# Expert stage of a fused two-layer kernel: first product in 512 columns, next expert's numbers read between blocks, output tiles signalled singly

## The reference

```python
cap = int(CAP_FACTOR * B * S / E)
t = x.reshape(-1, D)
probs = jax.nn.softmax(t @ Wr, axis=-1)
idx = jnp.argmax(probs, axis=-1)
...
ein = disp.reshape(E, cap, D)
h = jax.nn.relu(jnp.einsum('ecd,edf->ecf', ein, W1))
eout = jnp.einsum('ecf,efd->ecd', h, W2).reshape(E * cap, D)
...
x = x + jnp.tanh(g_ffn[1]) * _L1_ffn_ref(_layernorm(x, axis=-1), L1_ffn_Wr, L1_ffn_W1, L1_ffn_W2)
```

## Time and profile before

| | us |
|---|---|
| median of 3 runs | 2019.31 (2018.92 to 2020.88) |
| the profiled execution | 2018.42 |
| span of its profile | 2016.7 |
| TensorE busy | 1920.3 |
| VectorE busy | 953.5 |
| ScalarE busy | 742.3 |
| GpSimd busy | 759.5 |

### The profile page before, as it was taken

The page is one execution under the profiler, slowest core; times in us unless marked ns, Lnnn a source line. Parts: engine busy times, 40 slices in busy tenths (PEclk is TensorE's granted clock), DMA queues, the critical chain, the costliest instruction groups (busy, mean ns, idle before and its releaser), DMA issues.

```text
span 2016.7 us, 34799 instructions
## 1 busy us (share of the span) xinstructions
PE 1920.3 (95%) x10956; PEld 1630.0 (81%) x10957; DVE 953.5 (47%) x2245; ACT 742.3 (37%) x1711; POOL 759.5 (38%) x803
## 2 busy tenths in 40 slices
PE   5899999999999389999999999999999999999997
PEld 3677777777776279898899989998898998899986
DVE  6879999999985733324121332124133214121331
ACT  3446666666565322414111231124123114111331
POOL 5656675675652322415211241124224115211340
PEclk9999999999999699999999999999999999999999
DMA  7323443533534551505201250115124115101220
GB/s 241 110 87 126 158 148 126 174 132 126 183 122 166 169 174 55 175 29 171 76 27 35 65 169 26 36 42 173 52 72 157 31 32 183 52 31 31 92 75 11
DMA packets 152911, 208.79 MB, mean 104 GB/s; under 512 B 13472, under 2 KB 79264, under 8 KB 152839
## 3 DMA queue, kind: packets, MB, share of 16 engines
q1 hardware_dynamic: 111767, 114.15, 17.9%
q0 software_dynamic: 15728, 43.38, 7.1%
q10 hardware_dynamic: 25344, 50.33, 7.0%
HBM read 140.98 MB, written 68.37 MB: 104 GB/s over the span
## 4 chain that ended last, share of the span: by engine, by line
PE 82%; DVE 7%; issue 5%; ACT 1%; DVEq 1%; DMA 1%; POOL 1%; SPq 0%; ACTq 0%; POOLq 0%
PE bank L782 25%; PE bank L790 24%; PE bank L1527 7%; PE bank L1445 7%; PE bank L750 6%; PE bank L730 6%; PE bank L1499 2%; DVE x2T_lo L1855 1%; PE bank L708 1%; PE bank L739 1%; PE bank L1453 1%; DVE xdT_lo L1855 1%; DMA stage<-in_L_ffn_W_dram 1%; DVE a_m L1874 0%; DVE up_lo L1846 0%
## 5 line engine op out<-in xcount | busy, mean ns | idle before, releaser
L890 DVE SCALAR_TENSOR_TENSOR hT_lo<-bank,hT_hi 128x256 fp32r<-128x256 f32 x352 | 149.4, 424 | 678.6 <-ACT hT_hi L658 677.6
L658 ACT ACTIVATE hT_hi<-bank 128x256 fp32r<-128x256 f32 x352 | 134.9, 383 | 754.0 <-PE bank L782 744.5
L782 PE MATMUL bank<-inT_hi,w_hi 128*128 128x256 f32 x1408 | 399.7, 284 | 0.6 <-DVEq L938 0.6
L782 PE MATMUL bank<-inT_hi,w_lo 128*128 128x256 f32 x1408 | 400.0, 284 | 0.0
L782 PE MATMUL bank<-inT_lo,w_hi 128*128 128x256 f32 x1408 | 396.7, 282 | 0.0
L790 PE MATMUL bank<-w_hi,hT_hi 128*128 128x512 f32 x704 | 280.8, 399 | 0.0
L782 PEld LDWEIGHTS bank<-inT_lo,w_hi 128*128 128x128 f32 x1408 | 266.3, 189 | 14.5
L790 PE MATMUL bank<-w_lo,hT_hi 128*128 128x512 f32 x704 | 277.9, 395 | 0.0
L790 PE MATMUL bank<-w_hi,hT_lo 128*128 128x512 f32 x704 | 277.6, 394 | 0.0
L782 PEld LDWEIGHTS bank<-inT_hi,w_hi 128*128 128x128 f32 x1408 | 266.0, 189 | 13.9 <-DVEq L938 1.0
L782 PEld LDWEIGHTS bank<-inT_hi,w_lo 128*128 128x128 f32 x1408 | 265.2, 188 | 0.0
(11 more groups left out here) (314 smaller groups left out, 3805.3 us busy)
## 6 DMA issues: line engine op xcount, KB each, us to landing
stage<-in_L_ffn_W_dram SPq DMA_DIRECT2D x256, 256.0 KB, 3.0
X<-in_x_dram SPq DMA_DIRECT2D x16, 1024.0 KB, 5.7
t_d<-tt ACTq DMA_DIRECT2D x16, 1024.0 KB
x_d<-x ACTq DMA_DIRECT2D x16, 1024.0 KB, 6.7
out_dram<-y ACTq DMA_DIRECT2D x16, 1024.0 KB, 8.4
xs<-in_x_dram SPq DMA_DIRECT2D x16, 768.0 KB
cw_a<-in_L_xattn_conv_w_dram SPq DMA_DIRECT2D x2, 1024.0 KB, 10.0
cw_b<-in_L_xattn_conv_w_dram SPq DMA_DIRECT2D x2, 1024.0 KB, 15.0
```

The source lines that it names most:

```text
L658: act.activation(hT_hi[:, f % 4, :], hb[f % 4][:, 0:CN], ACT.Relu).then_inc(e_hh, 1)
L782: last = pe.matmul(hb[f % 4][:, 0:CN], l[:, k, fs], r[:, k, :], start=(n == 0), stop=(n == 3 * KB - 1))
L890: dve.scalar_tensor_tensor(out=hT_lo[:, f % 4, :], in0=hb[f % 4][:, 0:CN], scalar=0.0, in1=hT_hi[:, f % 4, :].bitcast(F32), op0=ALU.max, o ...
```

## The change

Three edits, all in the expert stage.

1. `inT_hi` and `inT_lo` become the two halves of one tensor `inT` [P, KB, 2, CN]. The first product multiplies w1_hi by both halves in one matmul of 512 columns, into the whole bank: hi by hi in the columns 0 to 255, hi by lo in the columns 256 to 511. The matmul w1_lo by inT_hi, 256 columns, adds to the second half. Per k two matmuls instead of three, 8 for a block; for the last k the short one comes first. ScalarE then copies the second half to `part` (two buffers, e_part), VectorE adds it to the first half, in place in the bank (e_sum), and relu and subtraction follow as before. On ScalarE `split_high` now stands between this copy and the relu.
2. TensorE's loop over the experts is written out in Python, and the four numbers of the next expert are loaded during the last chunk of the one before, at the blocks 3, 6, 9 and 12.
3. e_out is raised once for each output tile. In the last step of the kernel POOL waits for each tile on its own; elsewhere it waits for both.

```diff
-            inT_hi = eb("inT_hi", [P, KB, CN], F32R)
-            inT_lo = eb("inT_lo", [P, KB, CN], F32R)
+            inT = eb("inT", [P, KB, 2, CN], F32R)
+            inT_hi, inT_lo = inT[:, :, 0, :], inT[:, :, 1, :]
...
+            with nc.sbuf_tensor("part", [P, 2, CN], F32) as part:
+                pass
...
-                pool.wait_ge(e_out, all_c + 1)
-                settled(pool)
                 for i in range(CH):
+                    pool.wait_ge(e_out, all_c * CH + (i + 1))
+                    settled(pool)
                     put(ob[:, i, :], idx_x[:, i:i + 1], e_sc)
...
                     for f in range(FB):
                         act.wait_ge(e_m1, c * FB + f + 1)
+                        act.activation(part[:, f % 2, :], hb[f % 4][:, CN:2 * CN], ACT.Copy).then_inc(e_part, 1)
+                        if following is not None and f > BEHIND:
+                            split_high(following, f - BEHIND - 1, c)
+                        act.wait_ge(e_sum, c * FB + f + 1)
                         if f >= 4:
                             act.wait_ge(e_m2, c * FB + f - 3)
                         act.activation(hT_hi[:, f % 4, :], hb[f % 4][:, 0:CN], ACT.Relu).then_inc(e_hh, 1)
-                        if following is not None and f > BEHIND:
-                            split_high(following, f - BEHIND - 1, c)
...
                 def first_product(f):
                     fs = slice(f * P, f * P + P)
-                    n = 0
+                    both = hb[f % 4][:, :].rearrange("p (w c) -> p w c", w=2)
                     for k in range(KB):
-                        for l, r in ((w1_hi, inT_hi), (w1_hi, inT_lo), (w1_lo, inT_hi)):
-                            last = pe.matmul(hb[f % 4][:, 0:CN], l[:, k, fs], r[:, k, :], start=(n == 0), stop=(n == 3 * KB - 1))
-                            n += 1
+                        if k == KB - 1:
+                            pe.matmul(hb[f % 4][:, CN:2 * CN], w1_lo[:, k, fs], inT[:, k, 0, :], start=False, stop=False)
+                        last = pe.matmul(both, w1_hi[:, k, fs], inT[:, k, :, :], start=(k == 0), stop=(k == KB - 1))
+                        if k < KB - 1:
+                            pe.matmul(hb[f % 4][:, CN:2 * CN], w1_lo[:, k, fs], inT[:, k, 0, :], start=False, stop=False)
                     last.then_inc(e_m1, 1)
...
+                        if following is not None:
+                            if f == 3:
+                                begin_next = load(pe, unit_first[:, ds(following, 1)], MAXU)
+                            if f == 6:
+                                end_next = load(pe, unit_first[:, ds(following + 1, 1)], MAXU, 1)
+                            if f == 9:
+                                first_next = load(pe, chunk_first[:, ds(following, 1)], MAXC)
+                            if f == 12:
+                                last_next = load(pe, chunk_last[:, ds(following, 1)], MAXC)
...
-                with pe.Fori(1, E - 1) as e:
-                    begin, end = expert_units(pe, e)
-                    first_c, last_c = expert_chunks(pe, e)
+                begin, end, first_c, last_c = chunk(0, last_c, end, 1)
+                for e in range(1, E - 1):
...
-                    chunk(e, last_c, end)
+                    begin, end, first_c, last_c = chunk(e, last_c, end, e + 1)
...
                 def chunk(c, following=None):
                     for f in range(FB):
+                        dve.wait_ge(e_part, c * FB + f + 1)
+                        dve.tensor_tensor(hb[f % 4][:, 0:CN], hb[f % 4][:, 0:CN], part[:, f % 2, :],
+                                          ALU.add).then_inc(e_sum, 1)
                         dve.wait_ge(e_hh, c * FB + f + 1)
...
                     for i in range(CH):
-                        done = dve.scalar_tensor_tensor(out=ob[:, i, :], in0=acc[i][:, :], scalar=gp[:, i:i + 1],
-                                                        in1=xg[:, i, :], op0=ALU.mult, op1=ALU.add)
-                    done.then_inc(e_out, 1)
+                        dve.scalar_tensor_tensor(out=ob[:, i, :], in0=acc[i][:, :], scalar=gp[:, i:i + 1],
+                                                 in1=xg[:, i, :], op0=ALU.mult, op1=ALU.add).then_inc(e_out, 1)
```

More of the change, by code:

```diff
@@ L422, in flamingo_two_layers @@
             e_T, e_m1, e_m2 = sem("e_T"), sem("e_m1"), sem("e_m2")
+            e_part, e_sum = sem("e_part"), sem("e_sum")
             e_ih, e_hh = sem("e_ih"), sem("e_hh")
@@ L530, in chunk @@
                     chunk_inputs(c + 1)
-                    pool.wait_ge(e_out, c + 1)
+                    pool.wait_ge(e_out, (c + 1) * CH)
                     settled(pool)
@@ L792, in second_product, with chunk @@
                     last.then_inc(e_m2, 1)
-                def chunk(e, c, end):
+                def chunk(e, c, end, following=None):
+                    begin_next = end_next = first_next = last_next = None
                     for f in range(FB + BEHIND):
+                        if following is not None:
[7 more added lines that the diff above has]
+                                last_next = load(pe, chunk_last[:, ds(following, 1)], MAXC)
                         if f < FB:
@@ L807, in chunk @@
                             if f == BEHIND:
-                                pe.wait_ge(e_out, c + 1)
+                                pe.wait_ge(e_out, (c + 1) * CH)
                             second_product(f - BEHIND)
+                    return begin_next, end_next, first_next, last_next
                 pe.sem_inc(u_tr, NF)
@@ L823, in experts_on_tensor @@
                     chunk(0, c, end)
-                chunk(0, last_c, end)
-                with pe.Fori(1, E - 1) as e:
-                    begin, end = expert_units(pe, e)
-                    first_c, last_c = expert_chunks(pe, e)
+                begin, end, first_c, last_c = chunk(0, last_c, end, 1)
+                for e in range(1, E - 1):
                     with pe.Fori(begin, end) as u:
@@ L831, in experts_on_tensor @@
                         chunk(e, c, end)
-                    chunk(e, last_c, end)
-                begin, end = expert_units(pe, E - 1)
-                first_c, all_c = expert_chunks(pe, E - 1)
+                    begin, end, first_c, last_c = chunk(e, last_c, end, e + 1)
                 with pe.Fori(begin, end) as u:
                     unit(E - 1, u, first_c)
-                with pe.Fori(first_c, all_c) as c:
+                with pe.Fori(first_c, last_c) as c:
                     chunk(E - 1, c, end)
@@ L925, in experts @@
                     dve.sem_inc(u_out, 1)
-                    dve.sem_inc(e_out, 1)
+                    dve.sem_inc(e_out, CH)
                     for f in range(RING // 2, RING):
```

## The result

The changed kernel takes 1993.34 us (median of 4 runs, 1992.6 to 1994.73), the kernel before, timed beside it, 2020.1 us (2018.92 to 2021.02): ratio 0.9869, 95% interval 0.9852 to 0.9886. The profiled execution took 1992.6 us, its span is 1990.5 us, 26.2 us less than before.

A forecast was written before the change was run, and what follows sets the result against it. The prediction took TensorE's own stream, busy for 95% of the span, to bound the kernel. Terms of 12.7 us (products), 4.5 (boundaries) and 0.5 (output tiles) summed to 17.7 us less: 2001.6 us, range 1982 to 2017.

The forecast's parts named there:

- first rival: Expert stage: only removed matmul overhead counts, first product runs undisturbed; 23.7 us less in all, 1995.6 us, chance 0.25.
- likeliest case: Whole kernel: long matmuls of the first product disturbed at 233.3 ns; 17.7 us less, 2001.6 us, chance 0.37.
- First product: Expert stage: four long matmuls at 233.3 ns, four short at 120.0 take 1413 ns instead of 1440; 27 ns a block.
- Second product: Expert stage: its first matmul no longer follows a short one and falls from 240 to about 231 ns, 9 ns a block.
- rivals built on turns: Short-to-long turns in the expert stage: no first-product gain, 2014.3 us, chance 0.15; or 0.04 us a turn, 2023.8, chance 0.06.
- Helpers cost nothing: Expert stage: the new copy and add on ScalarE and VectorE stay hidden behind TensorE's work, costed at nothing.
- table of cover: Estimate between first and second product of a block: some 2.1 us of helper latency against 5.6 us of TensorE work.
- rival of the slow w_lo: Last chunks: VectorE's round passes the block if w_lo needs 1.4 us instead of 0.68; 2035 us at 1.8, chance 0.04.
- Reads: Expert boundaries: loading the next expert's four numbers between blocks removes TensorE's holes; 4.5 us, from 3 to 6.
- pieces called issue: Expert boundaries: chain pieces where TensorE stands still while its sequencer loads four numbers; six of them, 4.0 us in total.
- Instruction fetch: Expert loop written out: TensorE fetches five more copies of its body, costed at nothing.
- Output tiles: Kernel end: POOL starts after the first of two tiles, 0.7 us earlier, with a new 0.1 us wait; 0.5 us gained.

## Why the prediction was right, and where it was not

The direction, the range (1982 to 2017) and the place of the gain were right: the forecast had 17.7 us, 24.3 + 0.7 came. The result lies by the first rival (1995.6, chance 0.25), not by the likeliest case, whose own range (1998 to 2006) it misses. That it lies so near the rival is in part luck: the rival had 53 ns a block, all in the first product (18.7 us); 43 came there and 13 in the second product (18.5 us).

- **First product, 9.5 us forecast, 14.6 measured.** The term that was sized wrong is the price of a long matmul beside short ones. I took 233.3 ns, the mean of six long ones behind twelve short ones, for all four. The rows allowed 226.7. Measured is 1395 ns for the eight, 174.4 ns on average, where 226.7 and 120.0 would give 173.4: nearly undisturbed, 8 ns over. The overhead of 13.3 ns for each matmul, the same at 256 and 512 columns, carried the term.
- **Second product, 3.2 forecast, 3.9 measured, for a wrong reason.** The first long one behind a long one should fall from 240 to 231 ns. With a short one in front of it again, the second products got faster still, 1382 ns. The loss of 28 to 48 ns a block doesn't grow with the turns, and I had no right to count it for each turn. The rivals built on turns (2014.3 and 2023.8) fell with it.
- **Helpers cost nothing: right for their time, wrong for their latency.** The two kernels that differ by 704 helpers are equal to 0.01 us. The table of cover (5.6 us) asked when the matmul is due. It missed that the sequencer stands at the wait when it issues, more than 2 us ahead, and that reads and waits stand in program order behind it. With reads between blocks nothing stood there. In the changed kernel the omission cost nothing, because the second edit happened to move the reads; with the reads left at the head, the same reasoning would have been wrong by 5.8 us.
- **The rival of the slow w_lo** was ruled out by one short w_lo of one chunk. But "No row in a chunk has such a w_lo" was wrong for the trace: each of the seven last chunks of the kernel before has one of 2.6 to 3.5 us, and six of them another of 1.44, above the 1.4 that the rival needed. Once or twice in a chunk, it is hidden by two blocks of lead, and the round of the other blocks holds, so the rival fell, but not for the reason that I gave.
- **Reads, 4.5 forecast, 5.7 measured.** Two things were short: the pieces called issue (4.0 us) count less than the distances between starts, which shrank by 5.1 us; and the restart gave 0.6 us that I had put at nothing, after what I read out of the seventh boundary. From start to start the 24 matmuls took 5.57 to 5.59 us before and take 5.46 to 5.57 now. With the loop only written out, also without a hole, they take 5.49 to 5.58, so the hole alone does not decide it; what else does is open. That the reads themselves are hidden, and that e_il comes just in time, was right: distances are 0.23 us.
- **Instruction fetch, no cost:** right. The instruction queue has 62 packets instead of 41 (page), and TensorE is busy 1240.16 of 1240.20 us of the stage.
- **Output tiles, 0.5 forecast, 0.66 measured:** from the last matmul to the end of the span 12.77 us in the kernels with one signal for both tiles, 12.11 in those with one each.
- The 1.2 us left of the spans' difference lie in the token stage and are in no term.

The rule of the Trainium skill (TensorE: Matmul & The Clock Gate, "Back-to-back issue gap"), 2.5 ns for a warm matmul on top of its columns, would have given 3.5 us for the product. The section states it for an isolated matmul, and says that in a stream of pairs of weight load and matmul both set the distance, which the prediction left out. The runs have 18.5 us for 1408 matmuls, 13.1 ns each: here, with a weight load before each matmul, the rule does not hold. That the load is the reason is not shown, since no run goes without it.

## What to carry to other kernels

Where TensorE is full and each matmul has weights of its own, count matmuls as well as columns: here each cost 13 ns beyond its columns, and merging two moving operands that share weights into one of 512 columns paid even though it put a copy and an add on other engines. A longer chain behind a matmul is covered only if nothing else stands in TensorE's program behind the wait for it; move reads and branches away from there before lengthening it. To compare variants, measure a stretch between two instructions of the trace that repeats to 0.1 us, rather than a whole time with a stage in it that varies by 6.

## What was not expected of the hardware

- TensorE's waits are spent at issue, which ran 2.3 to 3.6 us ahead of the array at these boundaries (first load at 1390.8 for a stream that ends at 1393.82).
- A block of 14 to 18 matmuls loses 28 to 48 ns that neither widths nor turns explain; the amount depends on the order and repeats from block to block, or, in the changed kernel, every second block (2771 and 2795 ns in turn).
- A VectorE subtraction of 128x512 from the stages usually takes 0.68 to 0.85 us; one in every last chunk takes 2.3 to 4.9 us and ends 0.56 us after a subtraction of GpSimd. What holds it up was not tried.
- After 1.86 us without work and 1.3 us with it TensorE ran for 3.4 us at 1.2 GHz (512 columns in 0.43 us), but after 2.67 us without work at another place it did not.
